# A loop over three rounds written out in full, and one key mask added by eight products instead of sixteen

## What is computed

```python
scores = jnp.einsum('bhqd,bhkd->bhqk', qh, kh) * (1.0 / np.sqrt(D))
scores = scores * mask - (1.0 - mask) * NEG
attn = jax.nn.softmax(scores, axis=-1)
out = jnp.einsum('bhqk,bhkd->bhqd', attn, vh)
```

```python
cross_mask = jnp.broadcast_to(cpad[:, None, None, :], (B, 1, 1, S))
```

## Time and profile before

| | |
|---|---|
| median of 3 runs | 2357.57 us (2356.8 to 2361.8) |
| profiled execution, its own time | 2359.6 us |
| its span, first to last instruction | 2357.8 us |
| instructions in the trace | 100357 |
| busy share: PE, PEld, DVE, ACT, POOL | 94%, 78%, 78%, 71%, 59% |
| mean granted TensorE clock | 0.985 |

### The profile page before, as it was taken

How to read it: one execution, slowest core, us unless ns; L and a number is a source line. 1 busy time by engine, 2 the same in 40 slices (tenths; PEclk the granted TensorE clock), 3 DMA queues, 4 the chain that set the end, 5 groups by cost and what they waited for, 6 DMA issues and landing times.

```text
span 2357.8 us, 100357 instructions
## 1 busy us (share of the span) xinstructions
PE 2216.8 (94%) x37613; PEld 1837.2 (78%) x37613; DVE 1839.3 (78%) x4653; ACT 1682.8 (71%) x3278; POOL 1385.4 (59%) x3557
## 2 busy tenths in 40 slices
PE   2799999999999999999998999999999999999997
PEld 2688878788877887878887877777888878787876
DVE  3588887788777888878776888777877888887864
ACT  0477757788876775878886776677878877577876
POOL 3355446886554443888554544588756544388843
PEclk6899999999999999999999999999999999999999
DMA  6355455444444455444554545544455444544432
GB/s 149 100 138 131 125 135 131 115 121 126 126 124 114 127 129 137 125 114 116 131 132 109 133 126 132 141 114 122 120 129 130 121 117 115 137 126 115 119 100 59
DMA packets 310611, 289.39 MB, mean 123 GB/s; under 512 B 50080, under 2 KB 251552, under 8 KB 310112
## 3 DMA queue, kind: packets, MB, share of 16 engines
q1 hardware_dynamic: 305120, 279.80, 46.5%
q10 hardware_dynamic: 4128, 1.65, 0.4%
q0 software_dynamic: 864, 1.28, 0.3%
HBM read 130.51 MB, written 34.60 MB: 70 GB/s over the span
## 4 chain that ended last, share of the span: by engine, by line
PE 46%; POOL 23%; issue 21%; DVE 3%; DMA 2%; SPq 2%; ACT 2%; POOLq 1%; DVEq 0%; ACTq 0%
PE ps_scores_t L844 9%; PE ps_scores L807 6%; PE ps_out L832 5%; PE ps_turn L892 4%; PE ps_wide L914 4%; POOL x_bias L676 4%; POOL pre_rstd L618 2%; PE ps_wide L873 2%; PE ps_wide L872 2%; POOL post_rstd L618 2%; PE ps_turn L897 2%; PE ps_wide L882 2%; PE ps_out L903 2%; POOL post_normed L657 2%; PE ps_wide L911 2%
## 5 line engine op out<-in xcount | busy, mean ns | idle before, releaser
L1138 DVE TENSOR_REDUCE row_max<-ps_scores 128x16 f32<-128x1024 f32 x448 | 548.5, 1224 | 336.8 <-PE ps_scores L807 171.3
L746 ACT ACTIVATE probs<-ps_scores_t 128x512 f32<-128x512 f32 x896 | 535.1, 597 | 130.5 <-PE ps_scores_t L844 88.7
L1144 DVE TENSOR_TENSOR shifted<-ps_scores,row_max 128x512 f32<-128x512 f32 x896 | 577.4, 686 | 15.4
L844 PE MATMUL ps_scores_t<-ident,shifted 128*128 128x128 f32 x3584 | 567.6, 281 | 7.2 <-ACT probs L746 5.5
L844 PEld LDWEIGHTS ps_scores_t<-ident,shifted 128*128 128x128 f32 x3584 | 395.0, 142 | 54.3 <-issue 7.1
L736 ACT COPY pv_sb<-ps_out 128x256 f32<-128x256 f32 x448 | 167.7, 374 | 248.8 <-PE ps_out L832 247.4
L807 PE MATMUL ps_scores<-k_slots,qk_rows 32*64 32x256 f32 x7168 | 311.9, 401 | 26.1 <-issue 14.2
L832 PEld LDWEIGHTS ps_out<-probs,v_ones 128*32 128x32 f32 x14336 | 222.6, 110 | 140.8 <-issue 140.2
L832 PE MATMUL ps_out<-probs,v_ones 128*32 128x64 f32 x14336 | 294.6, 223 | 2.6 <-issue 1.3
L741 ACT ACT_TABLE_LOAD x190 | 243.8, 1283 | 3.4
L746 ACT ACT_TABLE_LOAD x189 | 242.5, 1283 | 3.4
(11 more groups left out here) (169 smaller groups left out, 4595.7 us busy)
## 6 DMA issues: line engine op xcount, KB each, us to landing
v_ones<-v_rows SPq DMA_DIRECT2D x1792, 64.0 KB
k_slots<-k_dram SPq DMA_DIRECT2D x448, 256.0 KB
k_dram<-qk_rows SPq DMA_DIRECT2D x448, 64.0 KB
x_in<-in_x SPq DMA_DIRECT2D x64, 64.0 KB, 1.9
ctx_in<-in_ctx SPq DMA_DIRECT2D x64, 64.0 KB, 1.9
out<-x SPq DMA_DIRECT2D x64, 64.0 KB, 1.6
k_dram<-zeros SPq DMA_DIRECT2D x4, 256.0 KB, 6.4
w<-in_L_xattn_W SPq DMA_DIRECT2D x2, 256.0 KB, 7.2
```

The lines of the kernel that those rows point to most:

```text
L746: nc.scalar.activation(probs[:, u, :, :], ps_scores_t[:, :] .rearrange("p (h t) -> p h t", h=4), ACT.Exp, scale=SCALE).then_inc(probs_read ...
L844: ins = nc.tensor.transpose(ps_scores_t[:, h * P:(h + 1) * P], shifted[:, j % 2, u, h * P:(h + 1) * P], ident[:, :])
L1138: v.tensor_reduce(row_max[:, :].rearrange("p (g n) -> p g n", n=SLOTS), ps_scores[:, :, 0:256].rearrange("p g (n k) -> p g n k", k=LEN), A ...
L1144: v.tensor_tensor(shifted[:, j % 2, u, :].rearrange("p (g n k) -> p g n k", n=SLOTS, k=LEN), ps_scores[:, 2 * u:2 * u + 2, 0:256].rearrang ...
```

## The change

`rounds` no longer makes a loop: one Python range runs over all phases from -6 to 471, and every engine's program is written out for the four rounds with constant waits and constant DRAM addresses. SP's phase takes round numbers from the unit numbers. In L2 cross, the mask is added by one group of 8 products in place of 16: the stationary operand `quad_first` has ones in the first of a group's 32 rows and zeros in the others, and the moving operand is the first half of the mask, whose first row is the key mask itself. Four DVE copies in the setup make `quad_first`. The causal masks are as before.

```diff
+        quad_first = sb("quad_first", [P, LEN], BF16)
...
-            if isinstance(r, int):
-                return dram[r, s]
-            return dram[bass.ds(r, 1), s, :, :].rearrange("r p c -> (r p) c")
-        BODY = range(FIRST, FIRST + PER_ROUND)
-        LAST = range(FIRST, PER_ROUND + LAG * STREAMS + DOWN + 2)
-        def rounds(eng, phase):
-            for j in range(-STATS, FIRST):
+            return dram[r, s]
+        PHASES = range(-STATS, UNITS + LAG * STREAMS + DOWN + 2)
+        def rounds(phase):
+            for j in PHASES:
                 phase(0, j)
-            with eng.Fori(0, ROUNDS - 1) as r:
-                for j in BODY:
-                    phase(r, j)
-            for j in LAST:
-                phase(ROUNDS - 1, j)
...
-                def phase(r, j, this, following):
+                def phase(r, j):
...
-                    if following is not None and i >= 0 and layer_of(i) == L0_SELF and in_program(i):
-                        load_next(r, i, following)
+                    if exists(r, i) and layer_of(i) == L0_SELF and round_of(i) + 1 < ROUNDS:
+                        load_next(r, i, round_of(i) + 1)
                     i = j - DOWN - 1
                     if exists(r, i) and layer_of(i) == L3_CROSS:
-                        store(r, i, this)
+                        store(r, i, round_of(i))
...
-                    if layer in MASK:
+                    if layer == L2_CROSS:
+                        for g in range(QUADS):
+                            of_g = slice(32 * g, 32 * g + 32)
+                            for b in range(2):
+                                ins = nc.tensor.matmul(ps_scores[64 * b:64 * b + 64, g, 0:256], quad_first[of_g, :],
+                                                       half_mask[of_g, 0, MASK[layer], :].unsqueeze(1)
+                                                       .to_broadcast([32, SLOTS, LEN]),
+                                                       start=False, stop=True)
+                    elif layer in MASK:
                         for half in range(2):
...
+                for g in range(QUADS):
+                    step(v.tensor_copy(quad_first[32 * g:32 * g + 32, :], ident[0:32, 0:1].to_broadcast([32, LEN])))
```

More of the change, by code:

```diff
@@ L577, in phase @@
                     i = j - FIRST
-                    if following is not None and i >= 0 and layer_of(i) == L0_SELF and in_program(i):
-                        load_next(r, i, following)
+                    if exists(r, i) and layer_of(i) == L0_SELF and round_of(i) + 1 < ROUNDS:
+                        load_next(r, i, round_of(i) + 1)
                     i = j - DOWN - 1
                     if exists(r, i) and layer_of(i) == L3_CROSS:
-                        store(r, i, this)
[L584 to L591, removed]
+                        store(r, i, round_of(i))
+                rounds(phase)
                 for s in range(STREAMS):
@@ L698, in phase @@
                         pre_norm_end(r, j + STATS)
-                rounds(pool, phase)
+                rounds(phase)
             @block.scalar
@@ L765, in phase @@
                         copy_turned(r, j)
-                rounds(act, phase)
+                rounds(phase)
             @block.tensor
@@ L977, in phase @@
                         turns(r, j)
-                rounds(pe, phase)
+                rounds(phase)
             @block.vector
@@ L1206, in phase @@
                         pre_norm_begin(r, j + STATS)
-                rounds(dve, phase)
+                rounds(phase)
 SETUP_RAW_T = 8
 SETUP_WIDE = SETUP_RAW_T + 9 + 11 + 4 + 3
-SETUP_BIAS = SETUP_WIDE + 4 + 12 + 10 + 1 + 11 + 1 + 3
+SETUP_BIAS = SETUP_WIDE + 4 + 12 + 14 + 1 + 11 + 1 + 3
 SETUP_DVE = SETUP_BIAS + 3 + 7
```

## The result

The changed kernel takes 2337.39 us (median of 4 runs, 2334.27 to 2339.3) against 2357.19 us before (median of 4), a ratio of 0.991 with a 95% interval of 0.9896 to 0.9923. The forecast was 2334.0 us in a range of 2325 to 2343. Its profiled execution took 2338.47 us, with a span of 2336.3 us; before it was 2359.6 and 2357.8. The kernel before ran again with each group of experiments, with medians of 2358.41, 2355.73 and 2361.04 us; so kernels of different groups are best compared by their ratios to their own runs of before.

A forecast was written before the change was run, and what follows sets the result against it. PE was taken to carry most of the chain, with idle time and slow clock at the loop's branches back. Branches -20.4, mask -4.0 and setup +0.85 make -23.6 us, from the median 2357.57 to 2334.0 us; range 2325 to 2343.

The forecast's parts named there:

- The branches: Loop's first two round ends, units 134 to 137: removing two branches back saves 11.40 + 9.01 = 20.4 us.
- none has work left to cover the others: At the round ends: all engines branch at the same phase, so the branches' whole 20.4 us counts.
- Code: Straight code over all rounds: instruction fetches, block crossings and the added POOL wait cost 0.
- The straight form fetches no more: Instruction fetch: the 6.65 MB already cover every instruction executed, so the amount stays the same.
- The mask: L2 cross units: eight mask products fewer save 4.0 us in all, with ends of 0 and 13.4 us.
- The price of 0.10 us per unit: Between scores and values of an L2 cross unit on PE: eight mask products fewer save 0.10 us.
- The count of ten units in sixteen: L2 cross units per round where the saving counts: five even before POOL's stretch, five odd after; 10 x 4 x 0.10 = 4.0 us.
- one of the forecast's own rivals: L2 cross mask gives nothing, POOL or the wait ahead of the values hiding the eight products: 2338.0 us, chance 0.16.
- Setup: Setup on DVE: four more casts of 32 x 64 cost 0.85 us, on the path.

The follow-up runs named there:

- one_branch: Changed kernel with a loop over two rounds and the third written out, so the branch back is taken once: 2348.77 us, ratio 0.9958.
- pe_loop: Changed kernel with only TensorE's program in the loop, the four other engines straight: 2363.89 us in one run.
- unroll_only: Changed kernel with the sixteen mask products back in L2 cross, still making quad_first in the setup: 2340.94 us, ratio 0.9932.
- pool_wait_off: Changed kernel with GpSimd's pre-norm wait for turns_ready only where the kernel before had it, outside the former loop: 2341.34 us in one run.
- the kernels with the slower norm: Changed kernel with subtract and multiply in one GpSimd instruction in norms behind L2's parts; eight mask products 2346.25 us, sixteen 2347.06 us.
- norm_in_one_no_mask: Changed kernel with subtract and multiply in one GpSimd instruction in norms behind L2's parts, and no L2 cross mask products: 2345.66 us.
- pe_straight: Changed kernel with TensorE's program straight and the four other engines in the loop: 2345.31 us in one run.

## Why the prediction was right, and where it was off

**The branches: right, to the hundredth in the profile.** The step that read them as 27.29 - 15.89 and 24.90 - 15.89 is confirmed by the changed kernel (three ends of 15.89), by `one_branch`, and by `pe_loop`. The price isn't fixed: six round ends with a branch of TensorE in four kernels cost 8.7 to 9.9 us, where one of the earlier trace rows cost 11.4. Two at their mean of 9.1 would have made the term 18.3 us, so that the exact match of 20.4 is a match with the one trace that the forecast was read from, and 2 us of it are that trace's luck. The reading "none has work left to cover the others" was half the truth: TensorE's gap is enough by itself, and the others' lie within it.

**Code: right in effect, wrong in its number.** The straight form costs nothing at crossings. "The straight form fetches no more" was too weak: `unroll_only` has 94312 instructions in its trace against 100357, 6045 fewer at the same work and four setup copies more, and the changed kernel fetches 0.7 MB less.

**The mask: the step that failed.** The price of 0.10 us per unit is exact (0.11 in units 88 to 96, 0.73 us against 0.83 in the timeline). The count of ten units in sixteen wasn't. It let the five even ones ahead of POOL's stretch count in full, as if PE set the pace wherever POOL doesn't. But in units 57 to 72 PE is busy for only 62.4 of 67.4 us, and among other things it waits for keys from DRAM, 6.3 and 9.1 us in four rounds, and in straight form no trace with fewer products was clearly shorter there. The five odd ones behind the stretch kept some half of their 0.5 us: of 0.44 us in units 88 to 96, 0.25 come back in the eight units after in the changed kernel, 0.15 in `pool_wait_off`. In units 72 to 104 of the four rounds the term measured 0.5 us in this pair of traces, 1.3 with `pool_wait_off` and 1.4 between the kernels with the slower norm. So of the 4.0 us, 0.5 to 1.4 are seen. Had it been left at nothing, one of the forecast's own rivals, 2338.0 us would have been the forecast, and 2337.39 the time.

**In range all the same.** The range reached up to a mask worth nothing, and that is where the time lies: the medians differ by 19.8 us, the two spans by 21.5, and the sum had 23.6. In the spans, a part of what the mask didn't give is made up by what no term had, 0.6 us in units 104 to 134 and 1.5 us at the two ends. That is luck.

**What no step had.** A wait made longer by a faster neighbour has a second price. The last wait for POOL was 1.57 to 1.59 us in the loop's rounds; with all engines in straight form it is 2.05 us, and 2.15 to 2.20 with eight products. Take the last such wait of each round in all runs that have them: the low clock followed none of the 11 that were 1.73 us or shorter, and 20 of the 37 of 2.04 us or longer, at 1.5 us each. Of the shorter waits ahead of them, one of 1.59 us in `norm_in_one_no_mask` was followed by it. The kernel before had one wait of 2.04 us or longer, the changed one has four.

**Setup: right.** The four casts take 0.83 us in the trace, for 0.85 forecast:

```profile
37.39 0.83 DVE L1039 CAST quad_first<-ident 32x64 bf16<-32x64 f32 x4
```

Whether they reach the end isn't shown. The first row maximum starts at 59.22 us, 0.6 us later than at 58.62, but among the kernels with the same setup it starts anywhere from 58.53 to 60.49.

**What stays open.** Why the first gap and the slow stretch were longer at the end that cost 11.4 us; what in a taken branch makes the gaps, since the trace names no releaser; how the form of a wait on TensorE moves single phases by some hundredths; and why PE's wait for keys in units 57 to 72 varies from round to round. No kernel here beats the changed one: with sixteen products its neighbour `unroll_only` is the same within its interval.

## What to carry to other kernels

If a kernel holds the same work in a loop and in straight code, compare the two inside one trace before anything is built: unit to unit in the body gives the price of the form, and the one round end that falls through gives the price of the branch. Take its size from more than one branch. Put a saving on one engine to account only after asking who paces the stretch; where another engine runs a backlog, the saving turns in good part into a longer wait, and where an engine also waits now and then for a transfer, what it saves can go into that wait. A longer wait of TensorE can cost clock besides. Before joining instructions on GpSimd, look at what the joined form costs, and before moving work to an engine with idle time, at what is queued behind it there.

## What the runs showed of the hardware

- A loop's branch taken on TensorE costs 8.7 to 11.4 us of this program, in two gaps (3.6 to 4.9 and 2.0 to 2.8 us) and 6.8 or 10.2 us at the lower clock. At the first end of `pe_straight`, on VectorE, ScalarE and GpSimd the gap is 3.0, 2.6 and 2.4 us; without TensorE's they cost 3.2 and 2.8 us at the two ends.
- The Trainium skill (Runtime: NRT & Kernel Launch, section Instruction fetch mechanics) says that a taken branch outside the window waits for a fetch, and that crossings in straight code are mostly hidden. The runs agree as far as they go: a gap at every branch taken, 15.89 to 15.92 us at every round end without one, and 5.96 MB of instructions fetched with one idle time of TensorE, 0.4 us, that has no releaser. That the gaps are the wait for the fetch, no trace names.
- On GpSimd a 128x128 instruction with two operations on fp32 and per-partition scalars takes 798 ns, one with a single operation and a broadcast operand 399 ns.
- TensorE came out of equal waits of 2.20 us twice at the full clock and twice at the lower one, which then lasted 3.4 us.
